# Expert gates kept in fp32 instead of three bf16 parts, router logits made per token, shared expert as a fifth inner chunk

## The reference

```
x = x + layernorm(attn(layernorm(x)))         # attn(y) = y + ripple(y)
x = x + layernorm(ffn(layernorm(x)))

# ripple: 8 heads of 16; each token attends to the tokens 0, 1, 2, 4, ... 512 behind it,
#         plus a 7-tap causal convolution of v, plus a linear attention (elu features); then @ Wo
# ffn:
scores    = sigmoid(x @ gate_W) * route_scale          # 8 experts
gate_full = the two largest scores of a token over their sum, zero for the other six experts
h         = gelu(x @ W1[e] + b1[e])                    # 8 experts, 64 inner channels each
y         = h @ W2[e] + b2[e]
out       = sum_e gate_full[e] * y[e]  +  gelu(x @ Ws1 + bs1) @ Ws2 + bs2
```

## Time and profile before

| | |
|---|---|
| runs | 341.28 us median (341.16 to 342.54) |
| profiled execution | span 339.5 us, first to last instruction; no time of its own beyond the span is given, the median of the runs is 1.8 us above it |
| PE busy | 261.4 us, 77% |
| DVE busy | 275.6 us, 81% |
| ACT busy | 176.8 us, 52% |
| POOL busy | 196.6 us, 58% |
| mean granted clock of TensorE | 0.874 of full speed |

### The profile page before, as it was taken

How to read it: one execution, slowest core, us unless ns; L and a number is a source line. 1 busy time by engine, 2 the same in 40 slices (tenths; PEclk the granted TensorE clock), 3 DMA queues, 4 the chain that set the end, 5 groups by cost and what they waited for, 6 DMA issues and landing times.

```text
span 339.5 us, 4554 instructions
## 1 busy us (share of the span) xinstructions
PE 261.4 (77%) x1527; PEld 175.7 (52%) x1527; DVE 275.6 (81%) x555; ACT 176.8 (52%) x443; POOL 196.6 (58%) x193
## 2 busy tenths in 40 slices
PE   6666667089379699997788499998795878888894
PEld 6323342087334537667455237767443277685374
DVE  5079866188999999989999999989999999845752
ACT  1683055302538755593569344775484606176852
POOL 4960999601889995306899980327979943131013
PEclk9785996569879959999999659999999559989999
DMA  7200376000025700200049300100248200000003
GB/s 219 71 0 16 106 196 147 24 0 3 9 90 143 215 26 8 69 26 3 37 130 229 111 12 2 31 2 8 84 124 215 83 12 31 0 2 0 2 2 93
DMA packets 20038, 21.89 MB, mean 64 GB/s; under 512 B 3289, under 2 KB 16434, under 8 KB 20014
## 3 DMA queue, kind: packets, MB, share of 16 engines
q1 hardware_dynamic: 20014, 21.59, 22.9%
HBM read 5.07 MB, written 2.10 MB: 21 GB/s over the span
## 4 chain that ended last, share of the span: by engine, by line
DVE 48%; PE 24%; ACT 9%; SPq 7%; DMA 6%; issue 4%; POOL 2%; POOLq 0%; DVEq 0%; ACTq 0%
DVE prods L263 12%; PE psH L1195 7%; DVE prods L880 6%; SPq L340 5%; DMA v_shift<-v_tok 5%; PE psA L1113 3%; DVE hid L994 3%; PE psY L1206 2%; PE psY L1292 2%; PE psA L1105 2%; DVE wgt L853 2%; PE psG L1278 2%; DVE gtmp L966 2%; SPq L339 2%; DVE gtmp L979 2%
## 5 line engine op out<-in xcount | busy, mean ns | idle before, releaser
L421 POOL TENSOR_SCALAR var<-ss 128x4 f32<-128x4 f32 (+1 forms) x25 | 13.4, 538 | 98.9 <-ACT squares L603 46.6
L263 DVE TENSOR_TENSOR prods<-qT,kT 128x1024 f32<-128x1024 f32 x32 | 55.4, 1778 | 12.4 <-ACT qT L530 12.4
L460 POOL TENSOR_TENSOR convT<-convT,tapT 128x1024 f32<-128x1024 f32 x24 | 57.9, 2412 | 2.0
L1195 PE MATMUL psH<-ident,prods 128*128 128x128 f32 x324 | 44.6, 290 | 0.0
L263 POOL TENSOR_TENSOR prods<-qT,kT 128x1024 f32<-128x1024 f32 (+1 forms) x12 | 28.8, 2418 | 23.2 <-PE psA L1163 11.3
L1195 PEld LDWEIGHTS psH<-ident,prods 128*128 128x128 f32 x324 | 40.5, 152 | 2.3 <-issue 2.3
L423 POOL TENSOR_TENSOR rstd<-var,neg_half 128x4 f32<-128x4 f32 (+2 forms) x29 | 37.8, 1305 | 2.4
L1163 PE MATMUL psA<-prods,slot_sel 128*32 128x512 f32 x168 | 26.0, 676 | 12.9 <-DVE prods L263 12.6
L880 DVE TENSOR_TENSOR prods<-v_shift,wgt 128x896 f32<-128x896 f32 x32 | 34.7, 1083 | 0.0
L880 DVE TENSOR_TENSOR prods<-v_tok,wgt 128x128 f32<-128x128 f32 (+2 forms) x60 | 25.8, 456 | 9.9 <-DMA v_shift<-v_tok 9.9
L1113 PE MATMUL psA<-xnT,wqkv 128*128 128x512 f32 x48 | 29.9, 767 | 5.0 <-ACT xnT L530 5.0
(11 more groups left out here) (194 smaller groups left out, 581.3 us busy)
## 6 DMA issues: line engine op xcount, KB each, us to landing
x_in<-L_attn_x SPq DMA_DIRECT2D x4, 512.0 KB, 4.0
x_res<-L_attn_x SPq DMA_DIRECT2D x4, 512.0 KB, 15.3
v_shift<-v_tok SPq DMA_DIRECT2D x4, 508.0 KB
v_shift<-v_tok SPq DMA_DIRECT2D x4, 504.0 KB
v_shift<-v_tok SPq DMA_DIRECT2D x4, 496.0 KB
v_shift<-v_tok SPq DMA_DIRECT2D x4, 480.0 KB
v_shift<-v_tok SPq DMA_DIRECT2D x4, 448.0 KB
out<-y_out SPq DMA_DIRECT2D x7, 256.0 KB, 2.3
```

The costliest lines, as they stand in the source:

```text
L263: return eng.tensor_tensor(prods[:, QUADS * (s % 2) + q, t0:T], qT[:, t0:T], kT[:, PRE - off + t0:PRE - off + T], ALU.mult)
L460: conv_chain(nc.gpsimd.tensor_tensor(convT[:], convT[:], tapT[:], ALU.add))
L1195: ins = pe.matmul(dst, terms[:, j % TERM_BUFS, m, :], ident[:], is_transpose=True, start=False, stop=(m == live[-1]))
```

## The change

1. DVE: steps 19 to 23 are gone. Step 18 writes fp32 gates to `gate_w` (two buffers, by unit). `identb` and its copy go too.
2. PE: the gate transposes are of 128x8 fp32 values with `ident`; `spread_gates` is an fp32 product of `gate_sel` (8x128) with the eight gate rows in `hid` chunk 4 (8x512).
3. ACT: the copy to `gT` is gone; `gate_rows` copies the eight turned rows straight from PSUM to `hid`. The copy to `gate_shared` is gone.
4. PE: the router's logits come from four small products a unit, `x3T` tile (128x128) as the stationary operand and `gw` (128x8) as the moving one, in token-major form at once; the product C4 and the four turns of logits go. In stages 1 to 3 the logits of u0 now stand behind `linear_state`.
5. The shared expert's inner rows come from a fifth product of `hidden` (chunk 4, L1256), after chunk 3; ACT's gelu for it reads PSUM. A unit still has seven uses of `psF` in stages 1 to 3: X3, LOGITS and five chunks. PE gives chunk 4 right after chunk 3 and before `low` for u0, and before tile 2 for u1.
6. Loads: `b2` once instead of three times, `gate_W` to a tensor of its own; 10 DMAs on `ffn_ld` instead of 12. POOL makes `gate_sel` with one instruction instead of three.
7. Last stage: the order of ACT and PE is written anew, `LAST_BANKS` and `LAST_GATE_STEPS` too.

```diff
-N_FRONT = 3
-N_HIDDEN = 4
-N_GATE_STEPS = 24
-LAST_BANKS = (0, 1, 2, 3, 0, 1, 2, 0)
-LAST_GATE_STEPS = (12, 15, 18, 21)
+N_FRONT = 2
+N_HIDDEN = CH
+N_GATE_STEPS = 19
+LAST_BANKS = (0, 1, 2, 3, 0, 1, 2, 0, 1, 2)
+LAST_GATE_STEPS = (10, 13, 15, 17)
...
-        gate_sel = sb("gate_sel", [24, 4, P], BF16)
+        gate_sel = sb("gate_sel", [EXPERTS, 4, P])
...
@@ ACT
-                copy(gate_shared[:, half_cols(u)], front(u, C4)).then_inc(front_free, 1)
...
-            def gates_expert_major(u):
+            def gate_rows(u):
                 act.wait_ge(gates_turned, u + 1)
-                copy(gT[:, u % 2, :], turned_gates(u)).then_inc(gT_ready, 1)
-            def gate_rows(u):
-                act.wait_ge(gT_ready, u + 1)
-                copy(hid[0:24, 4, half_cols(u)], gT[:, u % 2, :]).then_inc(shared_ready, 1)
+                copy(hid[0:EXPERTS, 4, half_cols(u)], turned_gates(u)).then_inc(gate_rows_ready, 1)
...
@@ DVE, gates
-                        ins = tt(g, both, spread(mrec), ALU.mult)
-                    elif n == 19:
-                        if u:
-                            dve.wait_ge(gates_turned, u)
-                        ins = copy(gparts[:, :, 0, :], g)
-                    elif n == 20:
-                        ins = tt(rest, g, gparts[:, :, 0, :], ALU.subtract)
-                    elif n == 21:
-                        ins = copy(gparts[:, :, 1, :], rest)
-                    elif n == 22:
-                        ins = tt(cand, rest, gparts[:, :, 1, :], ALU.subtract)
-                    else:
-                        ins = copy(gparts[:, :, 2, :], cand)
+                        ins = tt(gate_w[:, u % 2], both, spread(mrec), ALU.mult)
...
@@ PE
-                pe.matmul(front(u, C4), w1[:, 4 * P:5 * P], x3T[:, half_cols(u)], start=True, stop=True).then_inc(front_full, 1)
-            def turn_logits(u):
-                pe.wait_ge(front_free, upto(u, N_FRONT, 2))
                 for n, j in enumerate(unit_tiles(u)):
-                    ins = pe.transpose(front(u, LOGITS)[:, bass.ts(n, EXPERTS)], gate_shared[0:EXPERTS, bass.ts(j, P)],
-                                       ident[0:EXPERTS, 0:EXPERTS])
+                    ins = pe.matmul(front(u, LOGITS)[:, bass.ts(n, EXPERTS)], x3T[:, bass.ts(j, P)], gw[:],
+                                    start=True, stop=True)
...
-                    ins = pe.transpose(dst[:, bass.ts(n, P)], gparts[:, n].rearrange("p a e -> p (a e)"), identb[:])
+                    ins = pe.transpose(dst[:, bass.ts(n, P)], gate_w[:, u % 2, n, :], ident[:])
...
-                    pe.matmul(psG[:, c % 2, :], gate_sel[:, c, :], gT[:, u % 2, :], start=True, stop=True).then_inc(gate_spread, 1)
+                    pe.matmul(psG[:, c % 2, :], gate_sel[:, c, :], hid[0:EXPERTS, 4, half_cols(u)],
+                              start=True, stop=True).then_inc(gate_spread, 1)
...
@@ PE, stages 1 to 3
                     turn_scores(b)
                     if ffn:
-                        hidden(u0, (3,))
+                        hidden(u0, (3, 4))
                     low(b)
...
                             if j == 2:
-                                hidden(u1, range(2, 4))
+                                hidden(u1, range(2, CH))
...
@@ PE, last stage
-                    hidden(u0, range(2, 4))
+                    hidden(u0, range(2, CH))
                     gates_expert_major(u0)
                     spread_gates(u0, range(0, 2))
                     hidden(u1, (0,))
                     spread_gates(u0, (2,))
                     hidden(u1, (1,))
                     spread_gates(u0, (3,))
-                    hidden(u1, range(2, 4))
+                    hidden(u1, range(2, CH))
                     gates_expert_major(u1)
```

More of the change, by code:

```diff
@@ L132, in block_kernel @@
         ident = sb("ident", [P, P])
-        identb = sb("identb", [P, P], BF16)
         head_sel = sb("head_sel", [P, HEADS])
@@ L146, in block_kernel @@
         w1 = sb("w1", [P, CH * P])
+        gw = sb("gw", [P, EXPERTS])
         w2 = sb("w2", [P, CH, P])
@@ L203, in block_kernel @@
         x3T = sb("x3T", [P, T])
-        gate_shared = sb("gate_shared", [P, T])
         gexp = sb("gexp", [P, TPH, EXPERTS])
-        gtmp = [sb(f"gtmp{i}", [P, TPH, EXPERTS]) for i in range(10)]
+        gtmp = [sb(f"gtmp{i}", [P, TPH, EXPERTS]) for i in range(9)]
         gmax = [sb(f"gmax{i}", [P, TPH]) for i in range(6)]
-        gparts = sb("gparts", [P, TPH, 3, EXPERTS], BF16)
-        gT = sb("gT", [24, 2, HALF], BF16)
+        gate_w = sb("gate_w", [P, 2, TPH, EXPERTS])
         hid = sb("hid", [P, CH, T])
@@ L409, in more_constants @@
                     nc.gpsimd.memset(first_pref[:, :, e:e + 1], float(EXPERTS - e))
-                for part in range(3):
-                    v = gate_sel[:].rearrange("r c (a n) -> r c a n", a=2)
-                    nc.gpsimd.affine_select(out=v, in_=v, compare_op=ALU.not_equal, fill=1.0, base=-EXPERTS * part,
-                                            pattern=[[-2, 4], [-1, 2], [0, HID]],
-                                            channel_multiplier=1).then_inc(pool_set, 1)
-                    pool.wait_ge(pool_set, 4 + part)
+                v = gate_sel[:].rearrange("r c (a n) -> r c a n", a=2)
+                nc.gpsimd.affine_select(out=v, in_=v, compare_op=ALU.not_equal, fill=1.0, base=0,
+                                        pattern=[[-2, 4], [-1, 2], [0, HID]],
+                                        channel_multiplier=1).then_inc(pool_set, 1)
+                pool.wait_ge(pool_set, 4)
                 nc.gpsimd.memset(neg_half[0:1, 0:1], -0.5).then_inc(consts_ready, 1)
@@ L749, in _ @@
                     norm3_squares(u1)
-                    gate_logits(u0)
+                    gate_exps(u0)
                     normalise3(u1)
                     evacuate_x3(u1)
-                    gate_logits(u1)
-                    shared_hidden(u0)
-                    gates_expert_major(u0)
-                    hidden(u0, range(0, 4))
+                    gate_exps(u1)
+                    hidden(u0, range(0, 3))
                     gate_rows(u0)
-                    hidden(u1, range(0, 4))
-                    gates_expert_major(u1)
-                    shared_hidden(u1)
+                    hidden(u0, range(3, CH))
+                    hidden(u1, range(0, CH))
                     gate_rows(u1)
@@ L789, in centre_weights @@
                 dve.wait_ge(consts_ready, 1)
-                nc.vector.tensor_copy(identb[:], ident[:])
                 dve.wait_ge(wo_ld, 16)
@@ L1045, in _ @@
                     if ffn:
-                        gates(u0, range(4 if more else 2, 24))
+                        gates(u0, range(4 if more else 2, N_GATE_STEPS))
                     softmax_logits(b)
@@ L1055, in two_gate_steps @@
                             if ffn and j < TPH:
-                                gates(u1, range(2 * (3 * j + n), 2 * (3 * j + n + 1)))
+                                first = 2 * (3 * j + n)
+                                gates(u1, range(first, min(first + 2, N_GATE_STEPS)))
                         weigh(b, j, two_gate_steps)
@@ L1071, in _ @@
                 else:
-                    gates(u0, range(0, 24))
+                    gates(u0, range(0, N_GATE_STEPS))
                     done = 0
@@ L1388, in _ @@
                     gate_logits(u1)
-                    keep_busy(FILL_FRONT, spare)
-                    turn_logits(u1)
-                    hidden(u0, range(2, 4))
+                    hidden(u0, range(2, CH))
                     gates_expert_major(u0)
```

60 lines of the change are left out of this document (24 added, 36 removed).

## The result

| kernel | runs, us | ratio to before, 95% interval |
|---|---|---|
| before | 341.62 median (341.16 to 342.54, 4 runs) | |
| after | 359.98 median (358.67 to 362.06, 4 runs) | 1.0557 [1.0502, 1.0612] |

The runs of the kernel before are the three given above and one more. Where the runs of one kernel lie more than 1.5% apart, its ratio is worked out from the shorter ones.

What follows compares the result with a forecast made beforehand. The gating was taken as already near a PE bound, with PE the chain in the last stage. Stages 1, 2, 3 and last, +2.0 + 0.8 - 0.7 + 5.5 = +7.6 us, gave 341.3 + 7.6 = 348.9 us, range 341.5 to 355.5.

Steps and rivals of the forecast that it cites:

- Last stage: PE is the chain from the first spread; eight dearer spreads and u7's chunk 4 add 5.5 us.
- the 0.96 us slots: Last stage: each fp32 spread and chunk 4 holds PE 0.96 us; 8 x 0.65 + 0.96 = 6.2 us.
- rival 2: Clock stays at half through the spreads: stage 1 +6, stage 2 +3.1, in all +14, 355 us; chance 0.20.
- Stage 0: Fewer DMAs and cheaper constants are hidden by DVE's 9.91 us wait for `v_shift`: nothing.
- Stage 1: First half -0.7, half clock after PE's wait for chunk 4's bank +1.7, second half's PE work +1.3: rounded to +2.0 us.
- Stage 2: DVE's saved steps against PE's added work and clock falls: between -1.4 and +2.6, taken as +0.8 us.
- Stage 3: Gains before `weigh` become a wait for the shifted values' transfer; u1's saved steps against longer spreads leave -0.7 us.
- The lock that POOL hands on: DVE's L846, 1.55 us, takes over the port stall from the removed steps; without it stage 2 is 0.5 to 1 us lower.
- Rival 1: DVE decides and an 8-row fp32 spread holds PE under 0.4 us: -8, 333 us; chance 0.13.
- Rival 3: Clock never falls: stage 1 +0.6, stage 2 -1.4, stage 3 -1.0, last stage +4.5, sum +2.7, 344 us; chance 0.22.
- Rival 4: Transfer decides in all stages, gains and losses before `weigh` vanish: +8.4, 350 us; chance 0.45 together with the forecast.

Runs made afterwards that it cites:

- 64-row run: The changed kernel with fp32 spreads 64 rows deep instead of 8, the added selector rows zero: 351.34 us median, ratio 1.0358.
- `gw` last: The changed kernel with the small tile `gw` allocated after the last tile, the work the same: 355.77 us median, ratio 1.0453.
- 32 rows: The changed kernel with fp32 spreads 32 rows deep instead of 8, the added selector rows zero: 353.29 us median, ratio 1.0409.

## Why the prediction was right and wrong

**Last stage, +5.5 forecast, +14.4 measured: the step that failed.** The count was right. The first spread to the last product grew by 5.9 us of work at full clock (64-row run), against 6.2 by the 0.96 us slots and 5.5 taken; the price of a spread, 0.96 against 0.31 us, was right too. What failed is the clock. The prediction treated half clock as what follows idle time of PE, as 118.4 to 128.5 followed on 2.60 us of waiting, and since the last stage has no idle it gave it no fall in any case, not even in rival 2. The runs show that spreads of 8 rows bring half clock with PE busy 6.00 of 6 us and 9.00 of 9: 8.1 us. Deeper spreads with zeros, 32 or 64 rows, take it away in this stage: the four kernels with 8-row fp32 spreads all have 10 to 20 us of half clock in it, the three with 32 or 64 rows have none up to the last product. One row held a hint: half clock lasted on to 128.5 in stage 1, long after PE's 2.60 us of idle had ended at 117.5, and PE was doing spreads there.

By the Trainium skill (TensorE: Matmul & The Clock Gate, HAM oscillation — how this bites in real kernels) it is gaps in which TensorE stands idle that bring the lower clock, and keeping it fed is the remedy. The fall behind the 2.03 us wait in stage 1 is in line with that, though in the 64-row kernel PE waited the same 2.03 us (to 116.34) and the clock held until 133.2. The second fall in the last stage, at 342.0, is not in line: PE had stood idle last before 324.32. The first, at 328.3, followed 4 us behind a wait of 0.68 us, and with 64 rows the same wait brought no fall. There the measurement decides.

**Stage 0, 0 forecast, +2.25 measured.** I counted instructions and loads, and none of these moved the end. DVE's wait for the transfer ended 2.6 us later: 1.9 us are the longer transfer and 0.8 us its later start. The longer transfer goes with the tile `gw`: put last, it gives 40.8 us and a stage 0 of 86.02, and 32 unused bytes in the kernel before lengthen the transfer too. In part this stays open, since the bytes alone lengthened it by 1.1 us and not by 1.9. The start varied from 24.99 to 26.97 over the thirteen kernels, with the tile and without, so the 0.8 us aren't explained.

**Stage 1, +2.0 forecast, +3.46 measured.** The wait for chunk 4's bank was 2.03 us, forecast 2.0, and half clock from 116.7 to 120.1 was about the 3.3 us that the forecast took. But the forecast let both reach the end of the stage, and neither did. The table has four points in us after the stage's start:

| | before | changed | 64 rows | `gw` last |
|---|---|---|---|---|
| last product of u0's gates ends | 37.86 | 39.13 | 37.20 | 37.15 |
| POOL's last convolution step ends | 44.74 | 44.67 | 44.66 | 44.67 |
| first gate step of u1 | 44.81 | 44.74 | 44.73 | 44.74 |
| `experts_out` of u0 ends | 48.01 | 49.53 | 49.56 | 47.95 |
| stage ends | 70.78 | 74.24 | 74.28 | 72.66 |

At full clock the first half came out as forecast (-0.7), with the fall at +1.3 (forecast +1.0). Then DVE's first tile of `weigh`, a product with two SBUF inputs, met POOL's last convolution step and ended with it, whether it began at 43.1 or at 44.3:

```profile
129.45 2.35 POOL L460 TENSOR_TENSOR convT<-convT,tapT 128x1024 f32<-128x1024 f32 x1
131.87 0.17 DVE L935 TENSOR_SCALAR gtmp<-gexp 128x32 f32<-128x32 f32 x1
```
```profile
131.05 2.93 POOL L455 TENSOR_TENSOR convT<-convT,tapT 128x1024 f32<-128x1024 f32 x1
134.05 0.17 DVE L913 TENSOR_SCALAR gtmp<-gexp 128x32 f32<-128x32 f32 x1
```
```profile
131.65 2.35 POOL L455 TENSOR_TENSOR convT<-convT,tapT 128x1024 f32<-128x1024 f32 x1
132.41 1.74 DVE L858 TENSOR_TENSOR prods<-v_tok,wgt 128x128 f32<-128x128 f32 x1
```

(Kernel before, changed kernel, 64 rows.) So all of the 3.46 us lie behind this point, where the forecast had 1.3. 1.5 us are `experts_out`, ending later by the clock: in the changed kernel half clock from 126.9 to 133.8 made PE come to it 1.6 us late, with 64 rows half clock from 133.2 to 136.7 fell into it. The two kernels whose half clock lies elsewhere (`gw` last, 32 rows) have 72.66 and 72.61. The other 1.9 us are PE's added work behind it, sized at 1.3.

**Stage 2, +0.8 forecast, +0.85 measured.** Two large terms that nearly cancel. u1's first gate step began 45.70 us after the stage did, 2.25 earlier than before (47.95) and again where POOL's convolution ended (45.62), and behind it 3.1 us were lost. The forecast had -3.7 or -2.0 in front and +2.3 or more behind. PE's wait shrank from 6.19 to 1.57 us, and the clock fell from 198.6 to 208.9 behind the spreads. The close agreement is partly luck: the forecast was a value taken between -1.4 and +2.6.

**Stage 3, -0.7 forecast, -0.45 measured.** DVE was early and waited for the transfer, 3.23 us, which before it didn't:

```profile
281.02 0.86 DVE L858 TENSOR_TENSOR prods<-v_tok,wgt 128x128 f32<-128x128 f32 x1 [3.23 <-DMA v_shift<-v_tok]
```

From the first DMA at 239.64 that is 41.4 us, 40.4 in the forecast. The transfer is one limit of two: this tile ended at 281.88, and POOL's last convolution step at 281.73, as in stage 1.

**The lock that POOL hands on.** L824 (L846 before) lasted 1.76 us in stage 1, against 1.55. It began 29.1 us after the stage did (118.44 - 89.31), where L846 began 33.1 after (120.14 - 87.06): the 3.9 us of DVE's steps were saved up to there, and the stall that L824 took over is 0.2 us. The prediction had the right mechanism but named the wrong instruction: it is the first tile of `weigh` that met POOL's last step, and in stage 1 nothing of the 3.9 us was left behind it.

**Rivals.** Rival 1 (cheap spreads) falls by the 0.96 us. Rival 3 (no fall) falls by the two in stage 1. Rival 4 was right on the transfer in stage 3 only; in stage 1 what came before `weigh` did vanish, as it has it, but POOL's convolution decided that and not the transfer. Rival 2 was the nearest, 355: it had the clock at half through the spreads in stages 1 and 2, where little of it came, and not in the last stage, where most did.

## What to carry to other kernels

A product with few rows can be dear by TensorE's clock: where PE is the chain, look at the granted clock behind thin products, and try them with their rows filled up with zeros. That cost no time here and gave back 8.1 us with fp32 in the last stage; with bf16 it gave 1.1% of the kernel before. It did not hold the clock everywhere. DVE work that is taken away in stages where DVE decides doesn't pay for PE work added in the stage where PE does; sum by stage, and ask at each point of a stage which engine's end it meets: in stage 1 POOL's last convolution step swallowed what DVE had won and lost before it. And a new small tile is better put behind the large ones that DMAs copy, since it moves the addresses of all that follow.
